# Alternating PSUM targets of successive matmuls in a mixture-of-experts feed-forward kernel

## What is computed

```python
share_out = _gated_ffn(hidden_states, sWi0, sWi1, sWo)     # gelu(x @ wi0) * (x @ wi1) @ wo
hg = jax.nn.gelu(jnp.einsum('bsd,bdf->bsf', hidden_states, wi0), approximate=True)
hl = jnp.einsum('bsd,bdf->bsf', hidden_states, wi1)
expert_out = jnp.einsum('bsf,bfd->bsd', hg * hl, wo)
gate_in = jnp.concatenate([expert_out[:, 0], share_out[:, 0]], axis=-1)
weights = jax.nn.softmax(jax.nn.relu(gate_in @ g0) @ g1, axis=-1)
return expert_out * w0 + share_out * w1                    # plus x
```

## Time and profile before

| | us |
|---|---|
| median of 3 runs | 1979.04 (1978.45 to 1979.51) |
| the profiled execution | 1979.53 |
| its span, first to last instruction | 1977.8 |
| PE busy in the span | 1960.9 (99%) |
| DVE busy | 1525.3 (77%) |
| ACT busy | 1036.5 (52%) |
| POOL busy | 80.0 (4%) |
| DMA, mean over the span | 99 GB/s |

### The profile page before, as it was taken

The page is one execution under the profiler, slowest core; times in us unless marked ns, Lnnn a source line. Parts: engine busy times, 40 slices in busy tenths (PEclk is TensorE's granted clock), DMA queues, the critical chain, the costliest instruction groups (busy, mean ns, idle before and its releaser), DMA issues.

```text
span 1977.8 us, 29016 instructions
## 1 busy us (share of the span) xinstructions
PE 1960.9 (99%) x11158; PEld 1730.2 (87%) x11158; DVE 1525.3 (77%) x1819; ACT 1036.5 (52%) x1370; POOL 80.0 (4%) x56
## 2 busy tenths in 40 slices
PE   8999999999999999999999999999999999999997
PEld 7988888899998888889999888889999988888997
DVE  7777667789887666778988767668898976676886
ACT  5554344466566444446666644344666664444463
POOL 0010000002000000000101000000010100000000
PEclk9999999999999999999999999999999999999999
DMA  5431111244453111124445311112444531111342
GB/s 158 139 108 54 49 58 49 64 144 161 139 172 96 54 59 48 54 85 140 157 145 163 96 48 54 54 54 91 150 144 139 160 96 45 63 49 48 110 158 86
DMA packets 152412, 194.83 MB, mean 99 GB/s; under 512 B 10450, under 2 KB 116946, under 8 KB 150482
## 3 DMA queue, kind: packets, MB, share of 16 engines
q1 hardware_dynamic: 152274, 192.98, 31.0%
HBM read 184.55 MB, written 8.39 MB: 98 GB/s over the span
## 4 chain that ended last, share of the span: by engine, by line
PE 97%; DVE 1%; issue 0%; ACT 0%; DMA 0%; SPq 0%; POOL 0%; DVEq 0%; POOLq 0%; ACTq 0%
PE ps_out L415 35%; PE ps_pv L396 18%; PE ps_pv L406 17%; PE ps_c L396 14%; PE ps_c L406 13%; DMA a_src<-experts 0%; DVE al L808 0%; SPq L270 0%; ACT ah L586 0%; DVE a_src L827 0%; DVE s_out L1129 0%; SPq L279 0%; DVE xl L808 0%; DVE a_src L823 0%; DVE act L904 0%
## 5 line engine op out<-in xcount | busy, mean ns | idle before, releaser
L808 DVE TENSOR_TENSOR al<-a_src,ah 128x512 fp32r<-128x512 f32 (+2 forms) x289 | 401.1, 1389 | 39.0 <-ACT ah L586 35.2
L586 ACT CAST ah<-a_src 128x2048 fp32r<-128x2048 f32 (+2 forms) x285 | 336.7, 1193 | 3.2 <-DVE a_src L827 3.2
L396 PE MATMUL ps_pv<-xh,al 128*128 128x256 f32 x1024 | 290.0, 283 | 0.2 <-DVE act L940 0.2
L396 PE MATMUL ps_pv<-xl,ah 128*128 128x256 f32 x1024 | 289.8, 283 | 0.0
L396 PE MATMUL ps_pv<-xh,ah 128*128 128x256 f32 x1024 | 289.8, 283 | 0.0
L630 ACT ACTIVATE act<-ps_c 128x256 f32<-128x256 f32 (+1 forms) x192 | 87.5, 456 | 311.5 <-PE ps_c L396 174.2
L396 PE MATMUL ps_c<-xh,al 128*128 128x256 f32 x772 | 219.1, 284 | 3.8 <-DVE al L808 3.8
L396 PE MATMUL ps_c<-xl,ah 128*128 128x256 f32 x772 | 219.1, 284 | 0.0
L396 PE MATMUL ps_c<-xh,ah 128*128 128x256 f32 x772 | 219.0, 284 | 0.0
L685 ACT COPY ps_pv<-ps_c 128x512 f32<-128x512 f32 x127 | 72.5, 571 | 269.7 <-PE ps_c L406 182.1
L415 PE MATMUL ps_out<-wo0h,hidl 128*128 128x512 f32 x512 | 199.7, 390 | 0.8 <-DVE wo0l L808 0.8
(11 more groups left out here) (95 smaller groups left out, 3916.4 us busy)
## 6 DMA issues: line engine op xcount, KB each, us to landing
a_src<-experts SPq DMA_DIRECT2D x256, 256.0 KB, 3.8
raw_wo<-experts SPq DMA_DIRECT2D x128, 256.0 KB, 2.8
a_src<-shared SPq DMA_DIRECT2D x128, 256.0 KB, 3.0
g_sb<-g_rows SPq DMA_DIRECT2D x16, 1024.0 KB, 5.4
raw_wo<-shared SPq DMA_DIRECT2D x64, 256.0 KB, 2.8
x_src<-x_cols SPq DMA_DIRECT2D x32, 256.0 KB, 3.9
g_sb<-x_rows SPq DMA_DIRECT2D x7, 1024.0 KB, 4.9
out<-s_out SPq DMA_DIRECT2D x7, 1024.0 KB, 7.0
```

Of the source, the lines that this page charges most:

```text
L396: mm = nc.tensor.matmul(ps[:, a * HALF:(a + 1) * HALF], a_op[ap][:, i, a, k, :], x_op[xp][:, j, k, h, :], start=(start and a == 0 and k == ...
L586: nc.scalar.copy(a_op[HI][:, i:j, :, :, :], a_src[m % 2][:, i:j, :, :, :]).then_inc(a_hi_done, 1)
L808: nc.vector.tensor_tensor(to, of, hi.bitcast(F32), ALU.subtract).then_inc(done, 1)
```

## The change

In `product` the loop over gate and linear columns becomes the innermost, so that successive matmuls write to the two halves of the bank in turn. `down` takes two tiles, m and m + 1, and each pass is issued for one and then for the other; both tiles' increments of `down_done` sit on the last two matmuls. The callers go over pairs of tiles and wait for the buffers of both (m + 2 in place of m + 1). In the last down the wait for the first piece of the hidden values is gone; both pairs wait for both pieces. `wide_product`, and all engines but TensorE, stay as they are.

```diff
             def product(i, j, h, ps, start):
-                for a in (GATE, LIN):
-                    for k in range(2):
-                        for q, (ap, xp) in enumerate(PASSES):
+                for k in range(2):
+                    for q, (ap, xp) in enumerate(PASSES):
+                        for a in (GATE, LIN):
                             mm = nc.tensor.matmul(ps[:, a * HALF:(a + 1) * HALF], a_op[ap][:, i, a, k, :],
...
-            def down(m, s, start, stop, hidden):
+            def down(m, s, start, stop, hidden, done):
                 for f in range(2):
                     for q, (hp, wp) in enumerate(PASSES):
-                        mm = nc.tensor.matmul(ps_out[m][:, :], hidden[hp][:, f, m * P:(m + 1) * P], wo[s][wp][:, f, :],
...
+                        for i in range(m, m + 2):
+                            mm = nc.tensor.matmul(ps_out[i][:, :], hidden[hp][:, f, i * P:(i + 1) * P], wo[s][wp][:, f, :],
...
+                            if f == 1 and q == 2:
+                                mm.then_inc(done, 1)
...
-                    pe.wait_ge(added, (b // 2 + 1) * PAIR_ADDS - MC + (m + 1))
+                    pe.wait_ge(added, (b // 2 + 1) * PAIR_ADDS - MC + (m + 2))
...
-                    pe.wait_ge(out_copied, b * MC + (m + 1))
+                    pe.wait_ge(out_copied, b * MC + (m + 2))
...
-                    pe.wait_ge(added, b // 2 * PAIR_ADDS + row * MC - MC + (m + 1))
+                    pe.wait_ge(added, b // 2 * PAIR_ADDS + row * MC - MC + (m + 2))
...
                     for hb in range(2):
-                        for m in range(MC):
-                            shared_tile(m, hb, b - 1, n - 1)
+                        for m in range(0, MC, 2):
+                            shared_tiles(m, hb, b - 1, n - 1)
...
             pe.wait_ge(wo_ready, N_STEPS)
-            for m in range(MC):
-
-                pe.wait_ge(hid_ready, N_STEPS if m == 0 else N_STEPS + 1)
-                down(m, 1, False, True, last_hs).then_inc(last_down_done, 1)
+            for m in range(0, MC, 2):
+                pe.wait_ge(hid_ready, N_STEPS + 1)
+                down(m, 1, False, True, last_hs, last_down_done)
```

More of the change, by code:

```diff
@@ L410, in wide_product @@
                 return mm
-            def down(m, s, start, stop, hidden):
+            def down(m, s, start, stop, hidden, done):
                 for f in range(2):
                     for q, (hp, wp) in enumerate(PASSES):
-                        mm = nc.tensor.matmul(ps_out[m][:, :], hidden[hp][:, f, m * P:(m + 1) * P], wo[s][wp][:, f, :],
-                                              start=(start and f == 0 and q == 0), stop=(stop and f == 1 and q == 2),
-                                              skip_group_check=True)
-                return mm
+                        for i in range(m, m + 2):
+                            mm = nc.tensor.matmul(ps_out[i][:, :], hidden[hp][:, f, i * P:(i + 1) * P], wo[s][wp][:, f, :],
+                                                  start=(start and f == 0 and q == 0), stop=(stop and f == 1 and q == 2),
+                                                  skip_group_check=True)
+                            if f == 1 and q == 2:
+                                mm.then_inc(done, 1)
             hidden_of = [[t[:, h, :, :] for t in hs] for h in range(2)]
@@ L445, in c11_taken, with expert_tiles, shared_tiles @@
                     pe.wait_ge(product_done, products(t) + 1)
-            def expert_tile(m, b, n):
+            def expert_tiles(m, b, n):
                 c = n % STEPS
                 if c == 0 and b % 2 == 1:
-                    pe.wait_ge(added, (b // 2 + 1) * PAIR_ADDS - MC + (m + 1))
+                    pe.wait_ge(added, (b // 2 + 1) * PAIR_ADDS - MC + (m + 2))
                 elif c == 0 and b > 0:
-                    pe.wait_ge(out_copied, (b - 1) * MC + (m + 1))
-                down(m, n % 2, c == 0, c == STEPS - 1, hidden_of[0]).then_inc(down_done, 1)
-            def shared_tile(m, h, b, n):
+                    pe.wait_ge(out_copied, (b - 1) * MC + (m + 2))
+                down(m, n % 2, c == 0, c == STEPS - 1, hidden_of[0], down_done)
+            def shared_tiles(m, h, b, n):
                 row = n % STEPS * 2 + h
                 if row == 0:
-                    pe.wait_ge(out_copied, b * MC + (m + 1))
+                    pe.wait_ge(out_copied, b * MC + (m + 2))
                 else:
-                    pe.wait_ge(added, b // 2 * PAIR_ADDS + row * MC - MC + (m + 1))
-                down(m, n % 2, True, True, hidden_of[h]).then_inc(down_done, 1)
+                    pe.wait_ge(added, b // 2 * PAIR_ADDS + row * MC - MC + (m + 2))
+                down(m, n % 2, True, True, hidden_of[h], down_done)
             def expert_step(n, c, b):
@@ L506, in expert_step @@
                     for hb in range(2):
-                        for m in range(MC):
-                            shared_tile(m, hb, b - 1, n - 1)
+                        for m in range(0, MC, 2):
+                            shared_tiles(m, hb, b - 1, n - 1)
                 else:
                     of = b - 1 if c == 0 else b
-                    for m in range(2 if very_last else MC):
-                        expert_tile(m, of, n - 1)
+                    for m in range(0, 2 if very_last else MC, 2):
+                        expert_tiles(m, of, n - 1)
                 operands(P4)
@@ L516, in expert_step @@
                 if very_last:
-                    for m in range(2, MC):
-                        expert_tile(m, b, n - 1)
+                    expert_tiles(2, b, n - 1)
             def shared_turn(n, c, b, a):
@@ L542, in shared_turn @@
                     pe.wait_ge(wo_ready, n)
-                for m in range(MC):
+                for m in range(0, MC, 2):
                     if c > 0:
-                        shared_tile(m, a, b, n - 1)
+                        shared_tiles(m, a, b, n - 1)
                     elif a == LIN:
-                        expert_tile(m, b, n - 1)
+                        expert_tiles(m, b, n - 1)
                 if a == GATE:
```

## The result

| | before | after |
|---|---|---|
| median, us | 1979.04 (9 runs, 1978.45 to 1980.1) | 1984.46 (9 runs, 1984.16 to 1985.59) |
| ratio | | 1.0028, 95% interval 1.002 to 1.0036 |
| profiled execution, its span | 1979.53, 1977.8 | 1984.67, 1982.9 |

The changed kernel is 5.4 us slower. Of the 29 executions of the kernel before that stand beside the first four experiments, one took 3195.49 us at a mean granted clock of 0.57 and is not in their ratios.

What follows compares the result with a forecast made beforehand. TensorE, busy 1960.9 of 1977.8 us, bounds the kernel: only matmul distances, new TensorE waits and the serial end matter. 0 + 3.7 + 1.75 = 5.4 us on 1979.04 gives 1984.5 us, range 1980.5 to 1988.

Steps and rivals of the forecast that it cites:

- Part 1: In product and down, 7050 distances between matmuls change from same-place to alternating; expected gain 0 ns each.
- ends of 20 us either way: Bounds on the alternating distances in product and down: about 3 ns a change times 7050, -20 and +20 us.
- the surplus of 13 ns over streaming: 256-column matmuls stand 0.12 us apart against 0.107 of streaming; claimed to be there whatever the target is.
- Part 2: Tiles of down finish in pairs; TensorE waits for late buffers behind the shared pass, 4 x 0.92 = 3.7 us.
- the four places: Where an expert step follows the shared pass (c == 0 of the odd batches); 0.92 us each.
- the price behind a restart: After a TensorE wait in down, the next matmul comes 0.22 instead of 0.12 us later: 0.10 us.
- The parts counted at 0: Later tile ends in shared gate and lin turns and ScalarE's copies of expert tiles, claimed to be covered: 0 us.
- Part 3: At the last down, a later start (0.62 us) and tile 0's later end (1.13 us) lengthen the end by 1.75 us.
- The rival's picture: From a follow-up's forecast: the last down's later end is hidden behind the combining of the rows, 1984.5 us; no chance given.
- Rival A: Alternating in product and down gives time back: 0.8 ns a distance cancels the waits, 13.3 ns saves 94 us; chance 0.10.
- rival C: In product and down, alternation or the lost repeat of weights costs something, 1 ns a distance being 7 us; chance 0.06.
- Rival B: The waits behind the shared pass don't arise; the end alone is left, 1980.8 us; chance 0.08.

Runs made afterwards that it cites:

- the first four experiments: Kernel before with only product alternating, 1978.8 us; with only down paired, 1984.4; the change without its new waits, 1978.67; the change with two adds ahead of a_lo, 1981.33.
- the streams: Kernel before plus 24 runs of 48 matmuls behind its last down, varying width, target place, weights and type; ran once, 2135.01 us.
- the first and the third run: Kernel before with only product alternating, 1978.8 us; the changed kernel with two adds ahead of a_lo and the last down by tile, 1978.67 us.

## Why the prediction was right

**Part 1, 0 us.** It held. The step was to read the price of an alternating distance from the alternations that the kernel already had the earlier trace rows, although the printed step of 10 ns left ends of 20 us either way. (These ends were narrow: a printed step of 0.01 us over two changes of place is 5 ns each, which times 7050 is 35 us.) So the 0 was the likeliest reading of the rows and not proven by them; the middle stretches of the traces narrow it to 0.1 us for the whole kernel. The prediction left open where the surplus of 13 ns over streaming comes from and said only that the target does not matter; the streams bear this out.

**Part 2, predicted 3.7 us.** The mechanism, the four places and the late add are as the prediction put them, and the run with the adds ahead of a_lo takes this term away: its middle stretch is 1909.35 us, as in the kernels without the waits. The delay up to TensorE's restart measured 0.80 us and was forecast as 0.82 (869.97 - 869.21 + 0.06). The term that was mis-sized a little is the price behind a restart: 0.10 us was taken from one distance at the start, while the 24 matmuls behind the wait lose 0.18 us, since several distances and not one are longer. So a place costs 0.98 us where 0.92 was forecast, and four cost 3.9. The parts counted at 0 were 0: there is no wait in the shared turns. In the gate turn VectorE's last adds moved as expected. In the kernel after:

```profile
719.46 1.28 DVE L920 TENSOR_TENSOR s_out<-s_out,ps_out 128x512 f32<-128x512 f32 x2 [1.44 <-PE ps_out L417]
```

The last two adds now run as one block and end at 720.74, where the last one ended at 720.00; some 0.3 us of the difference is the whole program's shift by then, and nobody waits for them.

**Part 3, predicted 1.75 us.** Measured 1.83 us: 0.60 for the start of the last down, and 1.23 for tile 0's later end with the restart. The rival's picture, in which this end is hidden, does not hold: behind the copy both kernels need 14.9 us.

**The sum.** 5.4 us were forecast and 5.4 us measured between medians, but 5.8 us by the terms of the traces (3.94 in the middle and 1.83 at the end). The terms were thus forecast 0.3 us too small in all. That the medians agree to a tenth of a microsecond is luck, since the start alone scatters by 1.7 us from trace to trace. Rival A, from 0.8 ns a distance, is excluded by the first and the third run, rival C by the same. Rival B, that the four waits would not arise, is excluded by the trace of the changed kernel, which lists the four waits: VectorE ran a_lo and the adds without a gap and had nothing to close up.

## What to carry to other kernels

Before successive matmuls are reordered for the sake of their targets, look for a change of target that the trace already has and compare its distance with its neighbours'; if they are equal, expect nothing from more of them. The printed step of 10 ns times thousands of distances still leaves tens of microseconds open, and only a run that alternates without new waits closes that. Interleaving two results makes the first of them finish almost as late as the second and asks for both buffers at once, which was harmless in the long loops of this kernel and cost where the consumer has another long operation between two releases, or where the first result begins a serial tail. The stricter wait alone was free here, while together with the later end it was not.

## What the runs showed of the hardware that was not expected

At a granted clock of 1.00, fp32r matmuls of 256 columns stood 0.120 us apart and bf16 ones 0.109, against 0.107 us, which is half of the 0.213 us at a granted clock of 0.50. Whether the type makes this difference, or the zeros that the bf16 streams read, was not tested apart. Repeated weights did not shorten it. The Trainium skill, page "TensorE: Matmul & The Clock Gate", section "Back-to-back issue gap", gives N/2.4 + 2.5 ns; the bf16 streams agree with it to a nanosecond, the fp32r streams are 11 ns above it at 256 and 512 columns and 56 ns at 128.

For fp32r, 128 columns take 5.36 us for 48, 0.112 us each, hardly less than 256 columns, while bf16 halves (2.69 us, 0.056 each). The first 31 matmuls of 64 columns, up to 2094.06 us, started 0.112 us apart too. So fp32r had a floor near 0.112 us a matmul at full clock; that it is the weight load was not tested apart.

In the first stream of 64 columns the granted clock fell, though TensorE shows as busy throughout. Busy times of two stretches (PE, PEld, DVE, ACT, POOL, then the granted clock):

```profile
2080.00:2100.00 20.00, 20.00 (x204) 20.00 (x204) 0.00 (x0) 0.00 (x0) 0.00 (x0) 0.85 0.01 2
2100.00:2133.00 33.00, 32.95 (x231) 32.83 (x231) 0.00 (x0) 0.00 (x0) 0.00 (x0) 0.52 0.00 0
```

The clock was 1.00 up to 2094.0 us and 0.50, its lower level (1.2 GHz), from 2095.0 to 2128.5. It fell in the first 64-column fp32r stream, which followed the two 128-column bf16 streams, without an idle time of TensorE. In the last 1.3 us it was 1.00 again. So the 64-column streams say nothing about the place at full clock. At the lower level they do:

```profile
2097.88 10.43 PE L584 MATMUL ps_c<-xh,ah 128*128 128x64 f32 x48
2108.12 10.43 PE L586 MATMUL ps_c<-xh,ah 128*128 128x64 f32 x48
2118.36 10.43 PE L588 MATMUL ps_c<-xh,ah 128*128 128x64 f32 x48
2128.61 2.77 PE L590 MATMUL ps_c<-idle 128*128 128x64 bf16 x48
```

Two halves, two banks and one place with one set of weights take 10.24, 10.24 and 10.25 us for 48, 0.213 us a matmul, as long as 256 columns at this clock in the earlier trace rows.
